# Rows attention: value rows loaded from ScalarE's queue, two loads ahead of each of eight exponentials, instead of from SyncE's

## The reference, cut to what matters

```python
def _L2_attn_ref(x, wq, bq, wk, bk, wv, bv, wo, bo, gamma, beta):
    B, S, E = x.shape                      # 8, 256, 256
    H = NUM_HEAD                           # 16
    D = E // H                             # 16
    Q = x @ wq + bq
    K = x @ wk + bk
    V = x @ wv + bv
    Q = Q.reshape(B * H, S, D)
    K = K.reshape(B * H, S, D)
    V = V.reshape(B * H, S, D)
    scores = jnp.einsum('bqd,bkd->bqk', Q, K) / jnp.sqrt(jnp.float32(D))
    attn = jax.nn.softmax(scores, axis=-1)
    ctx = jnp.einsum('bqk,bkd->bqd', attn, V)
    ctx = ctx.reshape(B, S, E)
    out = ctx @ wo + bo
```

## Time and profile before

| | us |
|---|---|
| median of 3 executions | 2037.95 (2029.92 to 2040.02) |
| span of the profiled execution | 2036.8 |
| PE, DVE, ACT busy over the span | 1562.8, 1269.2, 779.2 |
| `project` of stage 3 ends, `attend` begins | about 702 |
| `attend` of stage 3 ends | about 920 |

### The profile page before, as it was taken

The page is one execution under the profiler, slowest core; times in us unless marked ns, Lnnn a source line. Parts: engine busy times, 40 slices in busy tenths (PEclk is TensorE's granted clock), DMA queues, the critical chain, the costliest instruction groups (busy, mean ns, idle before and its releaser), DMA issues. The chain is left out here.

```text
span 2036.8 us, 38838 instructions
## 1 busy us (share of the span) xinstructions
PE 1562.8 (77%) x13148; PEld 1212.7 (60%) x13148; DVE 1269.2 (62%) x2435; ACT 779.2 (38%) x1652; POOL 785.0 (39%) x956
## 2 busy tenths in 40 slices
PE   5958577649997587791285879947996999999990
PEld 3536464527774344461053546526886999999990
DVE  4846456566664665558224688675664777777776
ACT  2311012305453133451021336622114777777770
POOL 1531102360001440002222250014885887878770
PEclk8968788859998778895598879977997999999995
DMA  2465543354311633219331443114115656666545
GB/s 91 164 166 161 146 115 102 115 168 121 99 48 63 189 84 74 64 19 317 113 88 62 125 141 96 42 39 131 61 65 183 241 206 240 210 229 226 213 156 206
DMA packets 286766, 274.02 MB, mean 135 GB/s; under 512 B 59034, under 2 KB 263677, under 8 KB 280959
## 3 DMA queue, kind: packets, MB, share of 16 engines
q1 hardware_dynamic: 260535, 229.35, 36.3%
q10 hardware_dynamic: 17376, 21.31, 3.3%
q0 software_dynamic: 8688, 21.16, 2.8%
HBM read 194.74 MB, written 79.35 MB: 135 GB/s over the span
## 5 line engine op out<-in xcount | busy, mean ns | idle before, releaser
L787 DVE TENSOR_REDUCE a_maxima<-psum 128x2 f32<-128x512 f32 x384 | 257.5, 687 | 156.4 <-PE psum L578 88.7
L758 ACT ACTIVATE a_probs<-psum 128x512 f32<-128x512 f32 x384 | 224.6, 598 | 262.0 <-PE psum L600 167.8
L89 PE MATMUL psum<-e_x_split,e_up_split 128*128 128x256 f32 x2340 | 311.5, 282 | 7.4 <-DVE e_x_split L1749 7.4
L89 PEld LDWEIGHTS psum<-e_x_split,e_up_split 128*128 128x128 f32 x2340 | 292.5, 189 | 7.8 <-DVE e_x_split L1749 7.8
L1793 POOL TENSOR_TENSOR e_up_split<-e_up_raw,e_up_split 128x512 fp32r<-128x512 f32 x195 | 252.6, 1296 | 90.2 <-ACT e_up_split L1715 88.4
L1685 PE MATMUL psum<-e_down_split,e_hidden_split 128*128 128x256 f32 x1170 | 173.5, 284 | 0.4 <-DVE e_hidden_split L1775 0.4
L578 PE MATMUL psum<-s_k_stack,s_q_stack 96*128 96x256 bf16 x512 | 123.0, 295 | 41.6 <-DMA a_rel_stack<-scr_r 29.7
L1685 PEld LDWEIGHTS psum<-e_down_split,e_hidden_split 128*128 128x128 f32 x1170 | 152.5, 188 | 0.6 <-DVE e_hidden_split L1775 0.6
L1770 DVE TENSOR_TENSOR psum<-psum,e_silu 128x256 f32<-128x256 f32 x195 | 83.8, 430 | 106.8 <-ACT e_silu L1736 106.7
L1754 DVE TENSOR_TENSOR e_down_split<-e_down_raw,e_down_split 128x256 fp32r<-128x256 f32 x195 | 146.3, 750 | 0.0
L1039 DVE TENSOR_TENSOR a_products<-psum,mask 128x512 f32<-128x512 f32 x128 | 82.9, 686 | 78.6 <-PE psum L972 78.4
(11 more groups left out here) (247 smaller groups left out, 3178.1 us busy)
## 6 DMA issues: line engine op xcount, KB each, us to landing
e_up_raw<-in_w_ffn SPq DMA_DIRECT2D x39, 1280.0 KB, 7.4
e_down_raw<-in_w_ffn SPq DMA_DIRECT2D x39, 640.0 KB, 4.2
scr_q<-p_parts SPq DMA_DIRECT2D x40, 384.0 KB, 2.7
scr_k<-p_parts SPq DMA_DIRECT2D x40, 384.0 KB, 2.8
a_q_stack<-scr_q SPq DMA_DIRECT2D x96, 128.0 KB, 2.9
s_q_stack<-scr_q SPq DMA_DIRECT2D x96, 128.0 KB, 2.7
s_k_stack<-scr_k SPq DMA_DIRECT2D x96, 128.0 KB, 2.7
a_k_stack<-scr_k SPq DMA_DIRECT2D x84, 128.0 KB, 3.0
```

What stands on the lines that cost most here:

```text
L89: last = eng.matmul(out, lhs(a, k), rhs(b, k), start=i == 0, stop=i == len(terms) - 1)
L758: act.activation(PB[:, u % PR], st_bank(u), ACT.Exp, scale=0.25).then_inc(S["probs"], 1)
L787: dve.tensor_reduce(MX[:, u // 8, :, u % 8], s_bank(u), AX.X, ALU.max).then_inc(S["s_used"], 1)
```

## The change

`load_v` takes a range of the sixteen value loads, and every call of it moves from SP's list to ACT's. Image 0 is loaded in `project`, two loads after each of the eight activations of blocks 2 and 3. Image 1 is loaded at the head of ACT's list in `attend`. Image `i + 2` is loaded in step `i`, two loads ahead of the exponential of each unit from 8 to 15. ACT's loop now covers steps 1 to 5, and steps 6 and 7, which load nothing, are written out behind it. The numbers of loads, their sizes and their buffers are as before. SP also waits in `project` for the landing of the earlier value blocks before it writes the next.

```diff
-    def load_v(self, eng, scr_v, b):
+    def load_v(self, eng, scr_v, b, heads=range(HEADS)):
-        for h in range(HEADS):
+        for h in heads:
...
                     if scr_v is not None:
+                        if n:
+                            sp.wait_ge(v_spilled, 16 * n)
                         sp.wait_ge(v_ready, 2 * n + 2)
...
-                    if stacks is not None and scr_v is not None and n == 2:
-                        sp.wait_ge(v_spilled, 48)
-                        stacks.load_v(sp, scr_v, 0)
...
                             act.activation(feat(u, n), ps[:, u, :], ACT.Identity, bias=W["bias_qk"][:, u:u + 1]).then_inc(f_ready, 1)
+                            if scr_v is not None and n >= STEPS - 2:
+                                c = 8 * (n - STEPS + 2) + 2 * u
+                                if c == 0:
+                                    act.wait_ge(v_spilled, 16)
+                                stacks.load_v(act, scr_v, 0, range(c, c + 2))
...
-                    if rows and stacks:
-                        hold(S["v_copied"], index(i, 4, 4))
-                        load_v(i + 2)
...
-                    if rows:
-                        load_v(1)
...
-                def step(i, first=False):
+                def step(i, first=False, more=True):
                     for u in range(UNITS):
+                        if rows and more and u >= 8:
+                            if u == 8:
+                                act.wait_ge(S["v_copied"], index(i, 4, 4))
+                                act.wait_ge(S["v_loaded"], index(i, 256, 512))
+                            stacks.load_v(act, scr_v, i + 2, range(2 * (u - 8), 2 * (u - 8) + 2))
...
+                if rows:
+                    act.wait_ge(S["v_loaded"], 256)
+                    stacks.load_v(act, scr_v, 1)
                 step(0, first=True)
-                with act.Fori(1, IMAGES) as i:
+                with act.Fori(1, IMAGES - 2 if rows else IMAGES) as i:
                     step(i)
+                if rows:
+                    step(IMAGES - 2, more=False)
+                    step(IMAGES - 1, more=False)
```

More of the change, by code:

```diff
@@ L503, in hold @@
                     sp.sem_inc(S["sp_steps"], 1)
[L505 to L508, removed]
                 def stack(b):
```

## The result

| | before | after |
|---|---|---|
| median of 6 executions, us | 2037.69 (2029.92 to 2040.02) | 2023.55 (2023.04 to 2026.23) |
| span of the profiled execution, us | 2036.8 | 2021.6 |
| mean granted clock | 0.869 | 0.873 |

The ratio is 0.9934, with a 95% interval of 0.9917 to 0.9951. The change makes the kernel faster, by 14 us. The time lies inside the range; the gain is half of the 27.9 us that the sum gave.

The account below looks back on a forecast made before the run. SP's list of DMA issues was taken as the bound, its late placing stalling PE and lowering the clock. Gains of 38.9 us less 9.0 for ACT and 2 more left 27.9 off the span of 2036.8: 2010 as median, range 1997 to 2027.

Parts of the forecast that it names:

- The projection's end and the head: End of the projection: SP writes the last values without image 0's loads in front, 3.9 us gained before the barrier.
- The placing: Stage 3's attention: without value loads SP places the maxima before PE wants them at unit 8, with 2.3 us to spare.
- Gain of the five looped steps without ACT's cost: Steps 1 to 5, unit 8 to unit 8: down towards a clean step of 19.3 us, 24.5 us gained in sum.
- The step with the "issue" waits: Third of the five looped steps, 28.78 us: its "issue" waits stay, so it gives only 1.7 us.
- ACT's cost in these steps: Units 8 to 15 of the looped steps: two loads ahead of each exponential make ACT late, 1.5 us a step.
- Steps 0 and 1: From step 0 to unit 8 of step 1: 10.5 us gained without stalls and slow clock, before costs of 1.5 and 2.
- the signs that the prediction named: Trace after: clock 1.00 through steps 0 to 2, unit 8 to unit 8 20 to 22 us, exponentials about 1.4 us apart.
- A smaller gain of the same kind: Rival: stack loads land later, ACT's loop pays for code fetching, more "issue" waits; 16 us gained, time 2022, chance 0.16.
- The wait moves to ACT: Rival: each pair of loads waits for the exponential ahead to end; time 2040, no change, chance 0.08.
- The clock falls: Rival: ACT's pace gets PE only 1.2 GHz over most of a step; slower, time 2070, chance 0.06.
- The queue runs ahead: Rival: loads pass waiting exponentials and cost ACT nothing that PE sees; 36.9 us gained, time 2001, chance 0.2.
- The last point against the change: Skill's rule that several issuing engines save only small issue time; the prediction held it not small here, 9.86 us a step.

Follow-up runs that it names:

- e7: The changed kernel with the value loads of images 2 to 7 issued from POOL's queue, sixteen behind its copies of an image; 2002.69 us, ratio 0.9825.
- e8: The changed kernel with the value loads of images 0 and 1 back on SP, those of the steps still on ACT; 2028.35 us, ratio 0.9961.
- e3: The changed kernel without the value loads of images 2 to 7, the values of images 0 and 1 standing in; 2004.86 us, ratio 0.9838.
- e1: The changed kernel with the loads of a unit moved behind the context copies; 2010.24 us, ratio 0.9869.
- e5: The changed kernel with the two loads of unit 15 moved to unit 12, so four stand ahead of the context copy; 2031.0 us, ratio 0.9968.
- e2: The changed kernel with the sixteen loads of a step spread over units 6 to 10 and 13 to 15, none in 11 and 12; 2004.44 us, ratio 0.9828.

## Why the prediction came out half right

The sum had 27.9 us of gain, the traces show 15.48 up to step 6. The difference, term by term, with e7 as the kernel in which the loads of the steps disturb neither SP nor ACT:

- **The projection's end and the head: 3.9 forecast, 4.83 measured**, counted from the first values' write (in absolute times unit 0 is 5.24 earlier, of which 0.41 lie ahead). Against the start of DVE's last values, their write moved from 5.19 us behind to 1.35, 3.84 us, which is the term of the forecast, and the first scores of `attend` moved by 5.49 (14.25 to 8.76). What gives the 1.65 between the write and these scores is not shown. But image 0's loads beside ACT's activations were not free, as the forecast had them: DVE's last values come 33.64 us after the first write (33.64 to 34.02 in the eight kernels with these loads on ACT) and 32.99 before (33.00 in e8), so they cost 0.65 us.
- **The placing: right.** SP is early at every unit 8, and no wait for the placing is left.
- **Gain of the five looped steps without ACT's cost: 24.5 forecast, 22.28 in e7** (128.85 - 106.57). The four steps without the turn are right to 0.1 us. The step with the "issue" waits gave nothing instead of 1.7 (28.78 before, 29.46 in e7).
- **ACT's cost in these steps: 7.5 forecast (5 x 1.5), 15.07 measured** (after less e7: 3.51, 3.57, 4.67, 1.31, 2.01). This is the failed step: "ACT would be late by 1.7, of which the two PSUM banks take up to one unit, 0.9; I take 1.5 for each". The lateness itself was right in size: the waits at unit 12 are 2.40, 2.13, 2.17, 1.77 and 2.13 us, 0.45 of each is there in e3 and e7 too, so 8.35 us are new, 1.67 a step. That it meets the 1.7 is luck: the forecast had it from eight pairs of loads at 1.28 us each, at the end of the step, while a pair takes mostly 0.85 and the wait is there at unit 12, behind five pairs. Wrong were two things beside that price. PE hardly meets ACT through the banks of the scores, which would take some of it up (one wait of 0.41 us, in step 3), but head on, through the context copy that the loads stood in front of; e1 and e5, which only move loads around that copy, gain 13 us and lose 7. And there are 6.7 us more than the waits. In steps 1, 2 and 3, where the clock behind the wait is 0.72, 0.63 and 0.70, the step costs 1.56, 1.89 and 2.95 us more than its new wait; in steps 4 and 5, where the clock stays 1.00, nothing and 0.33. I had written of the kernel before that stalls cost more than their length, and had not applied it to the stall that I added.
- **Steps 0 and 1: 7.0 forecast (10.5 - 1.5 - 2), 3.03 measured.** Here ACT is only one of two. With ACT out of the way (e2, e7) PE waits 1.41 and 1.43 us for DVE, which the forecast had priced at 1, instead of 3.09 for ACT, and the stretch still takes 30.18 and 31.03 us. The forecast's floor was 24.0 (34.5 - 10.5); the best here is 26.64, in e3, where PE waits 1.67 us for DVE at the same place and the clock stays 1.00, against 0.50 in e2 (the last section has the windows). What decides that is not shown, and what would bring the last of it was not tried.

With these, 27.9 + 0.93 + 0.41 - 2.22 - 7.57 - 3.97 = 15.48. That the time still fell into the range is in part the width of the range: 14 us is half of the gain that was forecast. Of the signs that the prediction named, three more failed: the clock was not 1.00 through steps 0 to 2, the looped steps took 20.59 to 22.85 us (34.13 at the turn) and not 20 to 22, and the exponentials were 1.12 us apart and not 1.4.

**The rivals.** "A smaller gain of the same kind", 2022, gives the time, with twice the price a step as it said, but by another road than code loading. "The wait moves to ACT" named the right engine and the wrong reason and size: loads begin at an exponential's start, 0.17 us after it in step 1, not at its end. "The clock falls" through most of a step didn't come, though shorter falls did: it is 1.00 in 742 to 754 and 760 to 775 us. "The queue runs ahead" was wrong for exponentials that wait for their input and right elsewhere: a load passes activations whose input is there. In step 1 of the kernel after the load of 754.42 stands behind the copy of 754.51 and the exponential of 754.98, and begins before both. The Trainium skill says in "Perfetto Trace Analysis", section "DVE / Act Engine Instruction", that an instruction is handed to a wait queue with its wait and the sequencer is free then. By that rule loads would pass waiting exponentials too; the trace shows none that did.

The last point against the change was that issuing DMAs from several engines saves only the issue time, which is usually small (the Trainium skill, "DMA: Bandwidth & Descriptors", section "Issuing engines are not separate DMA queues"). Here it was not small: the sixteen issues of a step held SP for 9.86 us, and with them on POOL the three looped steps that ended in a long wait for the placing are 6.7 to 7.7 us shorter.

**What stays open.** How much a wait of a given length costs in clock: 2.13 us are followed by 0.63 in step 2 and by 1.00 in step 5. In the step of the loop's turn the three kernels with the longest waits at unit 12 take 34.13 (2.17), 32.21 (3.38) and 31.67 us (2.35), and those with less than 0.8 take 26.96 to 29.48; longer with a wait, but in no proportion to it.

## What to carry to other kernels

Moving DMA issues off a full queue is worth the stall that they caused, and costs the delay of what stands behind them on the new engine; so look on the new engine not for its busy share but for the one instruction that another engine needs at once, and put the loads behind it, never ahead. An engine that has slack nobody waits for (here POOL, at 0.62 us a load) is as good a home as one whose single issue is cheaper (ACT, 0.43 in a pair) with the loads placed by hand, and needs no such placing. And price an added stall as the trace prices the removed one, with the slow units behind it. Between two traces, count from an event just ahead of the change, not from the start: here that took some 6 us of scatter out of the first column.

## What the runs showed of the hardware

- In step 1 a load behind an exponential that had waited for its input begins 0.17 us after that exponential starts (0.46 for the first load of the step, which has two waits of its own, 747.73 against 747.27; in step 0 mostly 0.01 to 0.07). Behind activations that had not waited it begins up to 0.56 us before they do (754.42 against 754.98; in e1 751.95 ahead of the copy at 752.01).
- A pair of loads on ACT takes mostly 0.83 to 0.90 us, but some take much more: 2.20 at 727.13 in step 0 of the kernel after, 1.90 at 835.10. Why is not shown.
- The clock did not fall behind every wait of PE of this length. In step 0 of e2 a wait of 1.41 us for DVE is followed by 0.50, in step 0 of e3 one of 1.67 by 1.00 (windows, e2 and then e3, columns as in the earlier trace rows):

```profile
729.00:737.00 8.00, 7.96 (x102) 4.45 (x102) 5.01 (x8) 2.66 (x5) 0.41 (x2) 0.50 0.39 95
```

```profile
729.00:737.00 8.00, 7.09 (x148) 4.67 (x146) 6.10 (x11) 4.56 (x8) 0.83 (x4) 1.00 0.37 102
```

- The turn of PE's loop costs 3.5 to 4.2 and 1.0 to 2.1 us of "issue" waits in every changed kernel, and the clock over it is 0.61 (e7, 795 to 810 us) and 0.72 (e3, 788 to 800 us). At best, in e3, that step takes 7.7 us more than a clean one. It is the largest piece left in the looped steps; what causes the "issue" waits is not shown.
